# The second routing moved into the second mixture's block, with 14 of 32 key tiles projected beside it and the mask stored in eight pieces

## The reference, cut to what matters

```python
logits = xf @ gate_w.T + lb_bias
scores = jax.nn.sigmoid(logits.astype(jnp.float32))
topw, topi = jax.lax.top_k(scores, K)          # K = 2
topw = (topw / (topw.sum(-1, keepdims=True) + 1e-08)).astype(x.dtype)
for e in range(E):                             # E = 8
    m = topi == e
    sel = m.any(axis=-1)
    cnt = m.sum()
    wmean = (topw * m).sum() / jnp.maximum(cnt, 1).astype(topw.dtype)
    y = _mlp(xf, expert_gate_w[e], expert_up_w[e], expert_down_w[e])
    out = out + jnp.where(sel[:, None], y * wmean, jnp.zeros((), x.dtype))
out = out + _mlp(x, shared_gate_w, shared_up_w, shared_down_w)
```

## Time and profile before

| | us |
|---|---|
| median of 3 runs | 3079.47 |
| the runs | 3078.43, 3079.47, 5451.18 |
| the profiled execution | 3081.14 |
| its span, first to last instruction | 3079.3 |
| TensorE busy in it | 2774.2 (90%) |
| VectorE, ScalarE, GpSimd busy | 2031.7, 1840.5, 1428.6 |
| second routing's block | about 936.5 to 952.5 |
| second mixture's block | about 952.5 to 1107.7 |

### The profile page before, as it was taken

How to read it: one execution, slowest core, us unless ns; L and a number is a source line. 1 busy time by engine, 2 the same in 40 slices (tenths; PEclk the granted TensorE clock), 3 DMA queues, 4 the chain that set the end, 5 groups by cost and what they waited for, 6 DMA issues and landing times. The chain is left out here.

```text
span 3079.3 us, 70583 instructions
## 1 busy us (share of the span) xinstructions
PE 2774.2 (90%) x21912; PEld 2136.3 (69%) x21912; DVE 2031.7 (66%) x7995; ACT 1840.5 (60%) x5346; POOL 1428.6 (46%) x1748
## 2 busy tenths in 40 slices
PE   7999969986998989999999999988899984597999
PEld 5888854433766668888888777666677762386776
DVE  5445536664653456666666459999999999686433
ACT  5777734443543346666666468888888874453333
POOL 2122117762442434444444238787878786452000
PEclk9999979997998999999999899999999995697999
DMA  3000024323763311111111000000000000001000
GB/s 115 6 5 6 5 52 88 82 60 113 263 220 126 120 56 55 54 54 54 54 54 54 23 10 14 14 13 13 13 13 13 13 14 33 3 18 36 8 10 10
DMA packets 99461, 151.83 MB, mean 49 GB/s; under 512 B 11312, under 2 KB 39488, under 8 KB 98752
## 3 DMA queue, kind: packets, MB, share of 16 engines
q1 hardware_dynamic: 99296, 149.96, 16.5%
HBM read 103.33 MB, written 46.47 MB: 49 GB/s over the span
## 5 line engine op out<-in xcount | busy, mean ns | idle before, releaser
L1899 POOL TENSOR_TENSOR l2a_probs<-l2a_probs,l2a_inv 128x1024 f32<-128x1024 f32 x128 | 242.3, 1893 | 369.4 <-DVE l2a_inv L2065 369.2
L2010 ACT ACTIVATE l2a_probs<-l2a_s_ps,l2a_nm 128x256 f32<-128x256 f32 x512 | 236.6, 473 | 199.2 <-DVE l2a_nm L2041 199.2
L2847 DVE MAX8 l3a_top<-l3a_work 128x8 f32<-128x128 f32 x1536 | 314.2, 276 | 0.0
L2424 POOL TENSOR_SCALAR l3a_above<-l3a_score,l3a_top 128x128 f32<-128x128 f32 x504 | 294.1, 601 | 16.6 <-DVE l3a_top L2847 8.5
L2565 PE MATMUL l3a_l2o_ps<-net_arena 128*128 128x128 f32 x1952 | 256.1, 295 | 33.8 <-ACT net_l1f_gate L2681 33.4
L2565 PEld LDWEIGHTS l3a_l2o_ps<-net_arena 128*128 128x128 f32 x1952 | 249.6, 210 | 45.5 <-ACT net_l1f_gate L2681 37.0
L2849 DVE MATCH_REPLACE8 l3a_work<-l3a_top,l3a_work 128x128 f32<-128x128 f32 x1024 | 268.9, 275 | 0.0
L2552 PE MATMUL l3a_l2h_ps<-net_cols,net_arena 128*128 (+1 forms) x1024 | 251.9, 388 | 14.7 <-ACT net_arena L2716 12.8
L2552 PEld LDWEIGHTS l3a_l2h_ps<-net_cols,net_arena 128*128 128x128 f32 x1024 | 184.8, 191 | 67.2 <-ACT net_arena L2716 25.3
L721 ACT ACTIVATE l0a_probs<-l0a_score_ps,l0a_nm 128x128 f32<-128x128 f32 x512 | 180.1, 383 | 73.5 <-DVE l0a_nm L770 73.5
L2716 ACT ACTIVATE net_arena<-l3a_l2h_ps,net_l2f_b 128x256 f32<-128x256 f32 x496 | 203.6, 492 | 12.4 <-PE l3a_l2h_ps L2552 11.0
(11 more groups left out here) (532 smaller groups left out, 7152.6 us busy)
## 6 DMA issues: line engine op xcount, KB each, us to landing
kv_ahead<-l1a_kept SPq DMA_DIRECT2D x128, 256.0 KB, 2.7
l0f_code<-code_rows SPq DMA_DIRECT2D x32, 512.0 KB, 11.2
l2a_kT<-kv_ahead SPq DMA_DIRECT2D x64, 256.0 KB, 2.6
l2a_v<-kv_ahead SPq DMA_DIRECT2D x64, 256.0 KB, 2.6
l1a_shift<-neg_top SPq DMA_DIRECT2D x16, 512.0 KB, 4.9
l1f_chosen<-mask_code SPq DMA_DIRECT2D x64, 128.0 KB, 3.1
keys_ahead<-l1f_keys_kept SPq DMA_DIRECT2D x32, 256.0 KB, 3.2
l3a_kT<-keys_ahead SPq DMA_DIRECT2D x32, 256.0 KB, 2.7
```

Of the source, the lines that this page charges most:

```text
L1899: pool.tensor_tensor(p[:, :, :], p[:, :, :], per_row(inv[c % 2][a][:, :, :].rearrange("p i o -> p (i o)"), KV), ALU.mult).then_inc(scaled, 1)
L2010: act.activation(probs[c % 2][a][:, 2 * i + odd, :], s_ps[a][odd][:, i * KV:(i + 1) * KV], ACT.Exp, bias=nm[c % 2][a][:, i, odd:odd + 1], ...
L2424: ins = pool.tensor_scalar(above[:, i, :], score[c % 4][:, h, :], top[c % 2][:, ROUNDS - 1, h, 7:8], None, ALU.is_ge)
L2847: ins = dve.max(t[:, step // 2, h, :], src)
```

## The change

`l1_route` is gone. Its work is in `l1_mixture`'s block, with these differences:

- TensorE projects key tiles 0 to 5 first, then waits for the mask, then does for each of 8 groups the four transposes of the mask and one more key tile (6 to 13), with the sum matmul after group 2. The transposes use the banks of the output (`y_ps`), the sum uses `g_ps[0]`.
- ScalarE alone copies the turned mask, a group and a key tile in turn.
- SyncE stores the mask in eight pieces, each with its own semaphore, between key stores; after group 2 it issues the eight mask transfers of group 0, and it waits for the other seven pieces before the loop.
- In the loop groups 0 to 5 have three key tiles (c = 0 to 2), groups 6 and 7 none; before, groups 0 to 6 had four. A key store is issued in the step of its projection. There are 6 key buffers instead of 4.
- Layer (0,0) waits for VectorE's copy of the sum (`total_out`), outputs 0 and 1 wait until the mask is copied.
- The mixture's stage has 45 semaphores instead of 26.

The diff, cut (VectorE's choice moves word for word, but for the copy of the sum):

```diff
-def l1_route(nc, k):
...
+def l1_mixture(nc, k):
+    PAIRS, NC, RING = E // 2, E // 2 + 1, 4
+    FIRST_KEYS, LATER_KEYS = 14, 3
...
+        mask_kept = [s.sem(f"mask_kept{g}") for g in range(NG)]
...
-        keys = KeysAhead(s, k, range(NB), keys_ps, 4)
+        keys = KeysAhead(s, k, range(NB), keys_ps, 6)
...
+        def beside_mask(g):
+            return range(6 + g, 7 + g)
+        def key_beside(g, c):
+            i = FIRST_KEYS + g * LATER_KEYS + c
+            return i if c < LATER_KEYS and i < NB else None
         with nc.Block() as block:
...
-                sp.wait_ge(k.mask_out, 32)
-                for i in range(RING):
-                    load(i)
+                for i in range(6):
+                    keys.keep_one(sp, i)
+                for g in range(NG):
+                    cols = slice(g * BANK, (g + 1) * BANK)
+                    sp.wait_ge(mask_taken, g + 1)
+                    sp.dma_start(k.mask_code[:, cols], mask_rows[:, cols]).then_inc(mask_kept[g], 16)
+                    for i in beside_mask(g):
+                        keys.keep_one(sp, i)
+                    if g == 2:
+                        sp.wait_ge(mask_kept[0], 16)
+                        for i in range(RING):
+                            load(i)
+                for g in range(1, NG):
+                    sp.wait_ge(mask_kept[g], 16)
                 for i in range(NG * PAIRS):
-                    keys.keep_one(sp, i)
+                    key = key_beside(i // PAIRS, i % PAIRS)
+                    if key is not None:
+                        keys.keep_one(sp, key)
                     if i + RING < NG * PAIRS:
                         load(i + RING)
...
+                    if n == 0:
+                        pe.wait_ge(total_out, 1)
...
+                    else:
+                        pe.wait_ge(mask_taken, NG)
...
-                for i in range(PAIRS):
+                def turn_mask(g):
+                    if g >= 2:
+                        pe.wait_ge(mask_taken, g - 1)
+                    for j in range(G4):
+                        ins = pe.transpose(y_ps[g % 2][0:E, j * P:(j + 1) * P], mask[:, g * G4 + j, :], k.ident[:, :])
+                    ins.then_inc(mask_turned, 1)
+                for i in range(6):
                     keys.project(pe, i)
+                pe.wait_ge(mask_ready, 1)
+                for g in range(NG):
+                    turn_mask(g)
+                    for i in beside_mask(g):
+                        keys.project(pe, i)
+                    if g == 2:
+                        pe.wait_ge(part_ready, 1)
+                        pe.matmul(g_ps[0][:, 0:2 * E], k.ones[:, :], part[:, :, :].rearrange("p a e -> p (a e)"),
+                                  start=True, stop=True).then_inc(summed, 1)
                 for g in range(NG):
                     for c in range(NC):
                         layers(g, c)
                         if c == 2 and g >= 2:
                             turn(g - 2)
-                        if c < PAIRS and g + 1 < NG:
-                            keys.project(pe, (g + 1) * PAIRS + c)
+                        if key_beside(g, c) is not None:
+                            keys.project(pe, key_beside(g, c))
...
-                for i in range(PAIRS):
+                act.wait_ge(biased, 1)
+                act.activation(p[:, :, :], p[:, :, :], ACT.Sigmoid).then_inc(squashed, 1)
+                for i in range(6):
                     keys.take(act, i)
+                for g in range(NG):
+                    act.wait_ge(mask_turned, g + 1)
+                    act.activation(mask_rows[:, g * BANK:(g + 1) * BANK], y_ps[g % 2][0:E, :], ACT.Copy).then_inc(mask_taken, 1)
+                    for i in beside_mask(g):
+                        keys.take(act, i)
...
+                dve.tensor_copy(total[:, :, :], g_ps[0][:, 0:2 * E].rearrange("p (a e) -> p a e", a=2)).then_inc(total_out, 1)
+                dve.wait_ge(total_out, 1)
```

More of the change, by code:

```diff
@@ L1528, in _ @@
                             measure(n // 2 - 2)
-def l1_route(nc, k):
+def l1_mixture(nc, k):
+    PAIRS, NC, RING = E // 2, E // 2 + 1, 4
+    FIRST_KEYS, LATER_KEYS = 14, 3
     with ExitStack() as ctx:
-        s = Space(nc, ctx, "l1r", k)
-        rows = s.sb("rows", [E, NB * P])
+        s = Space(nc, ctx, "l1f", k)
+        mask_rows = s.sb("mask_rows", [E, NB * P])
         p, rest, eq, mask = (s.sb(n, [P, NB, E]) for n in ("p", "rest", "eq", "mask"))
@@ L1540, in l1_route @@
         red = s.sb("red", [P, NB])
[L1541 to L1610, removed]
@@ L1613, in l1_mixture @@
[L1613 to L1618, removed]
+        part, total = s.sb("part", [P, 2, E]), s.sb("total", [P, 2, E])
+        chain, biased, squashed, mask_ready, part_ready, mask_turned, summed, total_out, mask_taken = (s.sem(n) for n in (
+            "chain", "biased", "squashed", "mask_ready", "part_ready", "mask_turned", "summed", "total_out", "mask_taken"))
+        mask_kept = [s.sem(f"mask_kept{g}") for g in range(NG)]
@@ L1742, in _ @@
                             take_cols(g - 2)
-                        if c < PAIRS and g + 1 < NG:
-                            keys.take(act, (g + 1) * PAIRS + c)
+                        if key_beside(g, c) is not None:
+                            keys.take(act, key_beside(g, c))
                 take_cols(NG - 2)
@@ L1749, in _ @@
             def _(dve):
+                link = Chain(dve, chain)
+                k.l1r_w.wait(dve)
+                dve.tensor_tensor(p[:, :, :], k.logits[:, :, :], per_group(k.l1r_w.lb, NB), ALU.add).then_inc(biased, 1)
+                dve.wait_ge(squashed, 1)
+                top_two(link, dve, k, p, rest, eq, red, best, sel)
+                dve.tensor_tensor(mask[:, :, :], sel[0][:, :, :], sel[1][:, :, :], ALU.add).then_inc(mask_ready, 1)
+                dve.wait_ge(mask_ready, 1)
+                link(dve.tensor_tensor(red[:, :], best[0][:, :], best[1][:, :], ALU.add))
+                link(dve.tensor_scalar(red[:, :], red[:, :], 1e-8, None, ALU.add))
+                link(dve.reciprocal(red[:, :], red[:, :]))
+                link(dve.tensor_tensor(p[:, :, :], p[:, :, :], mask[:, :, :], ALU.mult))
+                link(dve.tensor_tensor(p[:, :, :], p[:, :, :], per_row(red[:, :], E), ALU.mult))
+                link(dve.tensor_reduce(part[:, 0, :], p[:, :, :].rearrange("p t e -> p e t"), AX.X, ALU.add))
+                link(dve.tensor_reduce(part[:, 1, :], mask[:, :, :].rearrange("p t e -> p e t"), AX.X, ALU.add))
+                dve.sem_inc(part_ready, 1)
+                dve.wait_ge(summed, 1)
+                dve.tensor_copy(total[:, :, :], g_ps[0][:, 0:2 * E].rearrange("p (a e) -> p a e", a=2)).then_inc(total_out, 1)
+                dve.wait_ge(total_out, 1)
+                link(dve.tensor_scalar(total[:, 1, :], total[:, 1, :], 1.0, None, ALU.max))
+                link(dve.reciprocal(total[:, 1, :], total[:, 1, :]))
+                link(dve.tensor_tensor(k.expert_weight[:, :], total[:, 0, :], total[:, 1, :], ALU.mult))
                 w.wait(dve)
```

3 lines of the change are left out of this document (1 added, 2 removed).

## The result

The median went from 3079.47 to 3067.99 us, 11.5 us less; the ratio is 0.997 (95% interval 0.9959 to 0.9981), that is 6 to 13 us. The forecast was 3068. That they agree within a tenth is luck: single runs of the changed kernel lie between 3063 and 3074 us, and the profiled one took 3074.13 (span 3072.3), only 7.0 less than the profiled one of before. The medians can't judge the terms of the sum; the distances inside one trace can. Up to group 7's last layer they repeat to 0.1 us between profiles of the changed kernel, so from here on times are counted from the start of the routing, VectorE's first operation on the logits (936.55 before, 937.17 after).

The account below looks back on a forecast made before the run. VectorE's chain was taken to bound the routing and TensorE the mixture, with a store stall in group 0. Terms 7.5 + 1.6 + 3.0 + 0.4 - 1.0 = 11.5 us took the median from 3079.5 to 3068; range 3063 to 3076.

Parts of the forecast that it names:

- Start: Routing: six tiles fit in the wait for the mask, eight rounds follow; layer (0,0) at 955.0 instead of 956.33, 1.3 us.
- Group 0: First mixture group: three steps of 2.61 plus a pair held to 4.01 make 11.84 us, against 17.96 before.
- The 5.8 us stall: Group 0 before the change: ScalarE's key copy waits for stores queued behind SyncE's mask loads, 5.8 us.
- The margins I stated: SyncE's queue up to group 1: key stores and mask load 4 land about 2 us before needed, costing nothing.
- Groups 1 to 5: Middle mixture groups with three key tiles: each saves 0.89 - 0.57 = 0.32 us, times five 1.6 us.
- The chain binds as said: c=3 to the next c=0: the product through ScalarE, GpSimd and VectorE needs 4.01 us, TensorE's work 3.44.
- Groups 6 and 7: Last mixture groups: group 6 loses all four tiles, 3.0 us; group 7 loses the wait for a late key copy, 0.4 us.
- The tail: Mixture's end after group 7's last layer: no term in the sum; clock dips there were named only for the range.
- Clears: Third layer's start: 19 more semaphores to clear at 0.055 us delay its first keys by 1.0 us; bounds 0 to 1.3.
- the stall in group 0: Rival, 18%: mask loads ahead of key stores stall group 0 again, 5.8 us back; gain 5.7, 3073.8 us.
- the chain was not free: Concerns a rival, 12%: the 0.57 us wait a group does not appear; gain 15.9, 3063.6 us.
- the clock rose 3.7 us into the tiles: Concerns a rival, 6%: TensorE stays at 1.2 GHz through the routing; kernel 2.7 us slower, 3082.2 us.

Follow-up runs that it names:

- a_best: Changed kernel with key tiles moved (six into the tail), semaphore clears moved to the end of SyncE's work, norm-weights wait behind the sigmoid; 3057.1 us, ratio 0.9924.
- a_six_after: Changed kernel with TensorE waiting for the mask before its first six key tiles; 3073.6 us, ratio 0.9999 to the kernel before.
- b_interleaved: Kernel before with six key buffers and SyncE alternating two mask loads and one key store; 3072.4 us, ratio 0.9982.
- a_keys_023: Changed kernel with each group's three key tiles behind layers c = 0, 2, 3 instead of 0, 1, 2; 3066.1 us, ratio 0.9965 to the kernel before.
- b_sems: Kernel before with 19 more, unused semaphores in the mixture's stage (45 in all); 3084.5 us, one run.
- a_clears_late: Changed kernel with the 45 semaphore clears at the end of SyncE's work in the third layer's attention instead of its start; 3060.2 us, one run.
- a_no_beside: Changed kernel without the eight key tiles between mask transposes, moved into groups 0 to 6; 3062.4 us, ratio 0.9954 to the kernel before.

## Why the prediction was right

Its steps, with their sizes:

- *Start: 1.3 forecast, 1.2 measured.* Right by two errors that nearly cancel. The mask came 0.54 us later than I took it: ScalarE's table load, which the kernel before began at the start of the block, begins in the changed kernel only when VectorE has added the bias (937.67; a_best, with the norm weights' wait moved, had it at the block's start and the mask 0.54 us earlier). And a round is 1.33, not 1.36 us, so that the rounds with the sum took 10.8 and not 11.1 us. (VectorE's chain up to the mask is 12 operations, not 14; the sum doesn't use their number.) a_six_after confirms that the waiting time is what was used.
- *Group 0: 11.84 forecast, 11.84 measured.* The 5.8 us stall was rightly sized and rightly put behind SyncE's queue; b_interleaved, with its two more buffers, gives all of it. The margins I stated held: no wait for a store or a mask appears, though load 4 left at 962.86 and not at 961.6. One margin I hadn't seen: the chain of layer c=0 takes 5.06 us here, against 5.22 of TensorE's work.
- *Groups 1 to 5: 1.6 forecast, 1.3 measured.* The chain binds as said (a_keys_023). Groups 2 to 5 are 16.82 and not 16.75 us: the layer matmul that has waited takes 1.10 and not 1.02 us in its row, and the next layer starts 0.08 us later; I had counted only the 4.01.
- *Groups 6 and 7: 3.4 forecast, 3.3 measured.*
- *The tail: 0 forecast, -0.3 measured.* From group 7's last layer to the next block 19.21 became 19.48 us, with the last output at 6.26 instead of 5.58 us. This stretch moved between 19.2 and 20.5 us in the ten profiles without tiles in it, from either kernel, with the clock in the last output, so the 0.3 isn't shown to be the change's; I had named it in the range only.
- *Clears: -1.0 forecast, -1.45 measured.* The mechanism was right (b_sems), the price per clear was taken too low: 0.08 and not 0.055, beyond the bounds that I read from two other blocks, where I had divided the whole delay by the count. Their difference, 0.42 us for six clears, is 0.07 each and would have given 1.3.

The sum of the measured terms is 10.3 us against 11.5. Nearly every term came out a little worse than forecast (only the round was shorter); the median hides that, as its interval is 7 us wide.

The rivals: the stall in group 0 didn't come, the chain was not free, and the clock rose 3.7 us into the tiles. The last was the only case on the other side, and the trace of before spoke against it. (The stretch from 927 that I called 8-column matmuls also has transposes of 128x128 in it, in turn with them; the case had that much more for it.)

What I weighed wrongly is where tiles are worth placing. I wrote that every tile in a middle group is paid in full and yet took the 14 tiles for one thing. Six are free, eight cost 0.56 us each where they stand, and the stillness of 3.9 and 4.6 us in the tail, in the same timeline of the kernel before, took six more for nothing:

```profile
1094.55 1.11 PE L1707 MATMUL l1f_y_ps<-net_ident,l1f_normed 128*128 128x128 f32 x4 [3.92 <-DVE l1f_normed L1778]
...
1105.65 1.12 PE L1707 MATMUL l1f_y_ps<-net_ident,l1f_normed 128*128 128x128 f32 x4 [4.61 <-DVE l1f_normed L1778]
```

## What to carry to other kernels

Before work is moved, list every place where the busiest engine stands still, with its length, and price a piece of work by what it pays in its old and in its new place; a wait for a two-step chain hides work too. A stall behind an issuing queue should be tested by changing the order on that queue first: here two more buffers and another order of loads and stores gave half of the gain. And whatever is added to a stage should be followed to the next one's first transfer, semaphores included.

## What the runs showed of the hardware

- *The same code takes different time in different runs.* The block "n1f" ahead of the routing is the same in all twelve profiles; it started between 907.0 and 916.8 us, and lasted 20.5 to 20.7 us in ten of them and 16.2 in two (a_six_after, a_clears_late). In those two TensorE's clock, which rises some way into the block, was up for 13.7 us, the last one of them in the next block; in the others it was up for 6.8 us and fell in the block's middle. This alone is 4 us between runs, as much as the effects under study.
- *Clears of semaphores* cost SyncE 0.08 us each (19 more than 26 took 1.5 us, b_sems), and stand in front of a stage's first transfer.
- *A late table load:* with a second wait placed ahead of the first activation, the load of its table began 0.5 us after the block's start; with that wait moved behind the activation it began with the block (a_best, 935.45). I had expected it to run ahead.
- *Transposes at full clock:* TensorE's granted clock was 1.00 through six us of nothing but transposes and one small sum (a_no_beside, 943 to 949).
